# Attention over edges: sums in batches of six over two PSUM banks, and the softmax head turned on VectorE

## What is computed

```
h = (x @ W_i).reshape(n, 4, 32)                     # 4 heads
e = leaky(es[src] + ed[dst])                        # one score per edge and head
m = segment_max(e, dst); p = exp(e - m[dst])
out = segment_sum(p / segment_sum(p, dst)[dst] * h[src], dst) + b_i
```

## Time and profile before

| | us |
|---|---|
| median of the timed executions | 10107.16 |
| the profiled execution's own time | 10027.24 |
| its span, first to last instruction | 10025.4 |
| PE busy | 5468.7 (55%) |
| DVE busy | 5313.1 (53%) |
| ACT busy | 4632.0 (46%) |
| POOL busy | 4936.8 (49%) |
| POOL gathers (L706) | 4980 instructions, 4700.9 busy, 3010.1 idle before them |
| PE sums (L1275) | 9984 instructions, 2452.2 busy |
| DVE adds (L1993) | 4992 instructions, 1476.5 busy |

### The profile page before, as it was taken

The page is one execution under the profiler, slowest core; times in us unless marked ns, Lnnn a source line. Parts: engine busy times, 40 slices in busy tenths (PEclk is TensorE's granted clock), DMA queues, the critical chain, the costliest instruction groups (busy, mean ns, idle before and its releaser), DMA issues.

```text
span 10025.4 us, 128907 instructions
## 1 busy us (share of the span) xinstructions
PE 5468.7 (55%) x33764; PEld 4402.8 (44%) x33764; DVE 5313.1 (53%) x12476; ACT 4632.0 (46%) x8410; POOL 4936.8 (49%) x5153
## 2 busy tenths in 40 slices
PE   3999799635444444553544445444534444444446
PEld 2777566524444444442444444444423333333334
DVE  5888711335555555554555555555634444444445
ACT  2555300245555555553555555555434444444444
POOL 2000300156666666662666666666466666666660
PEclk9999899855555555555555555555555555555558
DMA  2333355134333333442333333433322222222221
GB/s 83 141 135 141 122 187 191 61 99 108 102 103 101 103 103 103 107 105 66 102 103 102 102 102 104 108 102 103 80 74 76 71 71 71 76 71 71 71 76 32
DMA packets 600500, 985.16 MB, mean 98 GB/s; under 512 B 330886, under 2 KB 454492, under 8 KB 560780
## 3 DMA queue, kind: packets, MB, share of 16 engines
q1 hardware_dynamic: 216924, 540.94, 16.0%
q0 software_dynamic: 163376, 356.21, 15.2%
q10 hardware_dynamic: 219648, 81.82, 3.1%
HBM read 755.78 MB, written 222.74 MB: 98 GB/s over the span
## 4 chain that ended last, share of the span: by engine, by line
PE 30%; DVE 22%; another core or an unknown queue 19%; DVEq 14%; issue 10%; ACT 3%; DMA 1%; ACTq 1%; POOL 0%; POOLq 0%; SPq 0%
PE bank L1040 12%; DVEq L1363 11%; DVE acc L1993 10%; PE bank L1275 8%; DVE arena L1980 3%; PE bank L1064 2%; PE bank L1215 2%; PE bank L1203 2%; DVE bank L1949 2%; DVEq L1993 2%; DVE arena L1951 1%; ACT pick_dist L863 1%; DVEq L1985 1%; PE bank L1346 1%
## 5 line engine op out<-in xcount | busy, mean ns | idle before, releaser
L706 POOL DMA_INDIRECT arena<-row_table,staged_idx x4980 | 4700.9, 944 | 3010.1 <-issue 1749.0
L1275 PE MATMUL bank<-arena 128*128 128x136 f32 x9984 | 2452.2, 424 | 1521.3 <-issue 729.0
L1275 PEld LDWEIGHTS bank<-arena 128*128 128x128 f32 x9984 | 2171.8, 312 | 1688.3 <-issue 1688.2
L1993 DVE TENSOR_TENSOR acc<-acc,bank 128x136 f32 x4992 | 1476.5, 296 | 2096.8 <-issue 822.5
L863 ACT ACTIVATE pick_dist<-col,dst_local 128x128 bf16<-128x128 f32 x4992 | 1521.8, 388 | 551.1 <-remote 419.6
L1040 PE MATMUL bank<-arena 128*128 128x385 bf16 (+1 forms) x7448 | 1325.5, 327 | 36.5 <-DVE arena L1733 20.0
L815 ACT COPY x_mem<-bank 128x384 f32<-128x384 f32 x416 | 198.9, 478 | 1619.1 <-remote 1001.5
L1040 PEld LDWEIGHTS bank<-arena 128*128 128x128 bf16 x7448 | 702.2, 98 | 458.1 <-issue 22.1
L1980 DVE TENSOR_TENSOR arena<-arena,bank 128x528 f32<-128x528 f32 x1248 | 831.9, 687 | 0.7
L648 POOL TENSOR_TENSOR arena<-acc,node_stat 128x896 f32 x14 | 23.9, 1708 | 1612.6 <-POOLq L660 987.5
L1215 PE MATMUL bank<-ident,x_mem 96*128 96x96 f32 x1664 | 365.7, 375 | 738.7 <-DVE x_mem L1641 494.0
(11 more groups left out here) (371 smaller groups left out, 5343.6 us busy)
## 6 DMA issues: line engine op xcount, KB each, us to landing
arena<-dst_rows SPq DMA_DIRECT2D x156, 1024.0 KB
cell_rows<-arena SPq DMA_DIRECT2D x75, 1568.0 KB, 5.1
arena<-cell_rows SPq DMA_DIRECT2D x75, 1568.0 KB, 6.5
edge_stats<-x_mem ACTq DMA_DIRECT2D x416, 192.0 KB
arena<-row_table,staged_idx POOLq DMA_INDIRECT x4980
x_mem<-in_edge_attr SPq DMA_DIRECT2D x208, 192.0 KB
x_mem<-segment_flags SPq DMA_DIRECT2D x416, 96.0 KB
arena<-change_rows SPq DMA_DIRECT2D x312, 64.0 KB
```

The costliest lines, as they stand in the source:

```text
L706: pool.indirect_dma_start(gathered[:, at, :], None, table, bass.IndirectOffsetOnAxis(staged_idx[:, at:at + 1], 0)).then_inc(att_gathered[n ...
L1275: mm = pe.matmul(region(k)[:, 0:ROW], pick[:, k, :], gathered[:, b * GROUP + k, :], start=True, stop=True)
L1993: done = dve.tensor_tensor(row, row, region(m * BATCH + k), ALU.add)
```

## The change

Batches have six slots (the last one of a group two), so a group has 6 batches. Three sums lie side by side in a PSUM bank, a batch takes two banks, and two batches (`HELD`) are in flight, 12 sums in place of 8. All turns of the softmax head leave PE: they become 32x32 block transposes on DVE, and with them go five semaphore pairs and PE's places for them. `score_rows` and `back` stay in bank 3. The orders of PE and DVE are written anew for six batches.

```diff
-BATCH = 4
+BATCH = 6
+HELD = 2
+BANK_SUMS = 3
-    STEPS = GROUP // BATCH + 1
+    NBATCH = -(-GROUP // BATCH)
+    STEPS = NBATCH + 1
+        score_rows = bank[0:GROUP, 3, :]
+        back = bank[:, 3, 0:P].rearrange("p (h s) -> p h s", h=HEADS)
+        row_ends = over(3840, GROUP, 2 * GROUP)
+        cross_rows = over(3840 + 2 * GROUP, GROUP, 2 * GROUP)
-        def region(k):
-            return bank[:, 4 + k % (2 * BATCH) // 2, k % 2 * ROW:(k % 2 + 1) * ROW]
+        def slots_of(m):
+            return range(m * BATCH, min((m + 1) * BATCH, GROUP))
+        def region(G, m, k):
+            at = k - m * BATCH
+            spot = BATCH // BANK_SUMS * ((G * NBATCH + m) % HELD) + at // BANK_SUMS
+            return bank[:, 4 + spot, at % BANK_SUMS * ROW:(at % BANK_SUMS + 1) * ROW]
...
-                            act.wait_ge(att.summed, (n * NG + g + 2) * NBATCH + (q + 1) * (ROUND // BATCH))
+                            act.wait_ge(att.summed, (n * NG + g + 2) * NBATCH - (-((q + 1) * ROUND) // BATCH))
...
                 def sum_batch(G, b, m):
...
-                    pe.wait_ge(att.added, G * STEPS + m + FREE + (1 if m >= 2 else 0))
+                    taken_group, taken_batch = divmod(G * NBATCH + m - HELD, NBATCH)
+                    if taken_group >= 0:
+                        pe.wait_ge(att.added, taken_group * STEPS + taken_batch + 2)
...
                     for m in range(NBATCH):
                         sum_batch(G, b, m)
-                        if head and m == 2 + late:
-                            turn_scores(G + 1)
...
-                        if n < STATS_LAYERS and m in (4, 5):
-                            scan_turn(n, g, 0, m - 4)
-                        if ahead and m == 5:
-                            score_some(0, 2, slot, (G + 2) * 2)
-                        if ahead and m == 6:
-                            score_some(2, 5, slot, (G + 2) * 2)
+                        if n < STATS_LAYERS and m in (3, 4):
+                            scan_turn(n, g, 0, m - 3)
+                        if ahead and m == 4:
+                            score_some(0, 3, slot, (G + 2) * 2)
...
+                def turn_scores():
+                    then()
+                    for q in range(P // GROUP):
+                        dve.transpose(score_rows_h[:, :, q * GROUP:(q + 1) * GROUP],
+                                      score[q * GROUP:(q + 1) * GROUP, :, :])
+                    then()
...
+                    dve.transpose(row_ends[:, 0:GROUP],
+                                  seg_f_h.rearrange("s h e -> s e h")[:, ::-1, :][:, 0:GROUP // HEADS, :])
+                    dve.transpose(row_ends[:, GROUP:2 * GROUP],
+                                  seg_m_h.rearrange("s h e -> s e h")[:, 0:GROUP // HEADS, :])
...
+                    dve.transpose(cross_rows, cross[:, :, :].rearrange("p m s -> p (m s)"))
...
+                def turn_maxima():
+                    then()
+                    for q in range(P // GROUP):
+                        dve.transpose(back[q * GROUP:(q + 1) * GROUP, :, :],
+                                      seg_m_h[:, :, q * GROUP:(q + 1) * GROUP])
+                    then()
...
-                    late = 0 if ahead else 3
+                    late = 0 if ahead else 2
                     for m in range(NBATCH):
-                        if m + 2 < NBATCH:
-                            weigh(G, b, m + 2)
+                        if m + HELD < NBATCH:
+                            weigh(G, b, m + HELD)
                         add_batch(G, slot, m)
                         if head and m == 0 + late:
                             score_edges(G + 1, 1 - b, use)
                         if head and m == 1 + late:
-                            first_scans(G + 1, 1 - b, use)
+                            turn_scores()
+                            first_scans(1 - b, use)
                         if head and m == 2 + late:
-                            carries(G + 1, 1 - b)
+                            carries(1 - b)
+                        if head and m == 2 + late:
+                            last_scans(1 - b)
                         if head and m == 3 + late:
-                            last_scans(G + 1, 1 - b)
-                        if head and m == min(5 + late, NBATCH - 1):
-                            shift_scores(G + 1, 1 - b, slot + GROUP)
-                        if n < STATS_LAYERS and m in (2, 6):
+                            turn_maxima()
+                            shift_scores(1 - b, slot + GROUP)
+                        if n < STATS_LAYERS and m in (1, 4):
                             scan_edges(n, g, m // 4)
```

More of the change, by code:

```diff
@@ L1219, in _ @@
                 if n == 0:
-                    pe.sem_inc(att.added, FREE_REGIONS)
                     pe.sem_inc(st.turned, 2 * FREE)
@@ L1263, in score_some @@
                 def score_some(first, last, slot, turned):
+                    if first == 0:
+                        pe.wait_ge(att.scored, turned // 2)
                     for j in range(first, last):
@@ L1950, in last_scans @@
                     then()
-                    dve.tensor_tensor_scan(seg_m[:, ::-1], end_flag[:, b, ::-1], grp[:, ::-1], FAR,
-                                           ALU.add, ALU.max).then_inc(att.maxima, 1)
-                def shift_scores(head, b, slot):
-                    dve.wait_ge(att.max_back, head + 1)
+                    dve.tensor_tensor_scan(seg_m[:, ::-1], end_flag[:, b, ::-1], score_rows[:, ::-1], FAR,
+                                           ALU.add, ALU.max)
+                def turn_maxima():
+                    then()
+                    for q in range(P // GROUP):
+                        dve.transpose(back[q * GROUP:(q + 1) * GROUP, :, :],
+                                      seg_m_h[:, :, q * GROUP:(q + 1) * GROUP])
+                    then()
@@ L1956, in shift_scores @@
+                def shift_scores(b, slot):
                     dve.tensor_tensor(score[:, :, :], score[:, :, :], back, ALU.subtract
@@ L1989, in add_batch @@
                     dve.sem_inc(dve_tick, 1)
-                    for k in range(BATCH):
-                        row = acc[:, bass.ds(at[k], ROW)]
+                    for k in slots:
+                        row = acc[:, bass.ds(at[k - m * BATCH], ROW)]
                         then()
-                        done = dve.tensor_tensor(row, row, region(m * BATCH + k), ALU.add)
+                        done = dve.tensor_tensor(row, row, region(G, m, k), ALU.add)
                     done.then_inc(att.added, 1)
@@ L2001, in dve_group @@
                     rescale(G, slot)
-                    weigh(G, b, 0)
-                    weigh(G, b, 1)
-                    late = 0 if ahead else 3
+                    for m in range(HELD):
+                        weigh(G, b, m)
+                    late = 0 if ahead else 2
                     for m in range(NBATCH):
-                        if m + 2 < NBATCH:
-                            weigh(G, b, m + 2)
+                        if m + HELD < NBATCH:
+                            weigh(G, b, m + HELD)
                         add_batch(G, slot, m)
@@ L2024, in _ @@
                 score_edges(n * NG, 0, 0)
-                first_scans(n * NG, 0, 0)
-                carries(n * NG, 0)
-                last_scans(n * NG, 0)
-                shift_scores(n * NG, 0, 0)
+                turn_scores()
+                first_scans(0, 0)
+                carries(0)
+                last_scans(0)
+                turn_maxima()
+                shift_scores(0, 0)
                 for it in range(PAIRS - 1):
```

110 lines of the change are left out of this document (34 added, 76 removed).

## The result

The changed kernel takes 10583.04 us (10560.48 to 10595.91, four runs) against 10105.10 us for the kernel before in the same job: 1.0471 times as long, interval 1.0452 to 1.049. The forecast was 9920. The execution profiled took 10577.04 us (span 10575.0), 550 us more than that of before.

A forecast was written before the change was run, and what follows sets the result against it. It took POOL's chain of gathers with its pauses, not DVE's or PE's work, as the bound. Terms -1.5 + 0.1 + 0.2 = -1.2 us a group over 156 groups gave -187 us: 10107 to 9920 us, range 9590 to 10230.

The forecast's parts named there:

- The gathers' chain with its pauses: POOL's 32 gathers a group: 39.8 us plus 8.7 us of pauses make the whole 48.5 us period.
- rival B: Gathers' pauses fall to two a group, runs of 18 and 14: -3.3 us a group, 9590 us; chance 0.13.
- The waits of DVE for turns: DVE's waits for PE's two middle turns, 7.6 us a group, go; counted as no gain.
- The turns' price: Block transposes on DVE: 0.3 us large, 0.2 small; +3.8 us of DVE work a group, costing 0.2 us.
- 2.8 x 2.58 = 7.2 us against 8.7: POOL's pauses: 2.8 a group at 2.58 us each with batches of six, a gain of 1.5 us a group.
- told-late result of PE: PE results late in a gather run are seen only after its last gather, then about 2.6 us of nothing.
- A longer run covers it: Moved scan and turns delay DVE's adds up to 4.5 us; a 15 us run of 12 gathers covers PE's queued batch.
- The weight of 0.06 for DVE's work: Each microsecond of DVE work a group, beside the gathers, adds about 0.06 us to the period.
- the second weighing: Weighing at a group's start, half as long again: DVE's first add about 1.1 us later, counted as 0.1 us.
- one for the head: Softmax head's turns moved from PE to DVE: +3.8 us of DVE work a group, counted as 0.2 us.
- Rival C: DVE sets the pace, with turns, scans and adds in one line: 50.0 us a group, 10340 us; chance 0.20.
- The prediction's last sentence: Signs of being wrong; the last is a pause over 2.6 us because DVE, not the hold, ends it.

The follow-up runs named there:

- e1_turns: Kernel before with only the softmax head's block transposes moved to VectorE, batches of four and before's places kept: 1.0014 of the kernel before.
- e2_quarters: Changed kernel with five quarters of scores behind batch 4 and three behind the second edge scan's turn, instead of three and five: 1.0318 of the kernel before.
- e3_scans: Changed kernel with the second edge scan behind batch 3 instead of 4, the first scan's turns behind batches 2 and 3: 1.0204 of the kernel before.
- e4_both: Changed kernel with the edits of e2_quarters and e3_scans together: 1.0098 of the kernel before.
- e13_fixed: Changed kernel with adds to 32 fixed rows, so no address loads or register steps ahead of them (output not the reference's): 1.0083 of the kernel before.
- e10_late: e1_turns with the second edge scan's turns behind the next group's batches 0 and 1, their ScalarE copies ahead of its first picks: 0.9917 of the kernel before.
- e9_cut: e4_both with a pause on GpSimd (three small memsets, each behind a drain) behind every eighth gather: 1.0840 of the kernel before.
- e7_half: Changed kernel with every second gather of a group left out (output not the reference's), a trace only: period 42.2 us a group in the first layer.

## Why the prediction was wrong

*The part that held.* The gathers' chain with its pauses sets the period: in each kernel with all its gathers the period is 39.8 us and the pauses. Pauses became fewer, 2.1 a group, nearly rival B's two, with the runs of 18 and 14 that B names. The waits of DVE for turns are gone. The turns' price was right: 0.316 to 0.322 us for the large ones (0.3 taken), 0.177 to 0.222 for the small (0.2), DVE's busy time up by 30.0 - 27.0 = 3.0 us a group. The Trainium skill (VectorE: DVE Perf Modes, The three transpose paths and The TRN2 errata) gave 0.29 by the prediction's estimate; the trace has a tenth more. In e1_turns that work cost +0.14%, as little as forecast.

*The step that failed* is the first of the change, "2.8 x 2.58 = 7.2 us against 8.7": a pause's length was taken from before as if it were a constant, and only their number was let vary. The measured product is 2.1 x 6.6 = 14 us in the first two layers and, over the third, some 2.2 x 3.9 = 8.6, where it was 8.5. The rows show that length varying. By the starts in the earlier trace rows the pauses at 3314.56 and 3326.80 stand behind runs of 8 gathers and are 2.2 and 2.3 us over the 0.30; the one at 3350.16 stands behind a run of 16 and is 3.4. The prediction took every run for one of 8 ("a run is 8 gathers") and the mean of 2.58 for each. In the changed kernel's third layer, with runs of up to 18 and 24, the mean was 3.9, and that alone ate up the gain. The loss comes on top, in the pause of 9.7 us at gather 0 of the first two layers. What the pauses hold is no longer a told-late result of PE but an operand that isn't made: the sums of batch 3 in the pause of 3.9 us wait for adds that came late, and the next group's first sums in the pause of 9.7 us for the adds, the scan and its turns.

*"A longer run covers it"* (behind the moved steps: PE's batch after next, "which the longer run (15 us for 12 gathers) covers") was wrong too. The run is not neutral cover. In the changed kernel the steps of the very work that it is to cover are slow towards its end.

*The weight of 0.06 for DVE's work* came from comparing layers of the kernel before, where VectorE has few long steps. In e1_turns it held, 4.4 us more issue time a group for 0.5 us; in the changed kernel 9.8 us more went with 5.1 us. Work is cheap where it lies under the gathers, and lateness at the group's end is not.

*A place not priced.* The prediction had a term for the second weighing and one for the head, none for the second edge scan's move from 28 slots to 30 and for the two more quarters between its turns. e2_quarters and e3_scans give the two 1.5 and 2.7 points, with the slow adds in place.

*Rival C* was on the right side with the wrong mechanism: DVE did not run out of time, it is idle for 23.6 of 53.6 us; it was slow to issue. The prediction's last sentence names the sign that appeared, a pause "longer than 2.6 us since DVE, not the hold, ends it", but no case was made of it and no chance given. Its sum is off as well: 40.3 + 5.1 + 2 x 2.6 is 50.6 us, not 50.0, so by its own terms C stood at some 10435 us, not 10340.

*Open.* Why a run of gathers slows other engines' steps isn't shown, nor why VectorE's are spared in the runs of 16 of the kernel before. Whether the held results of PE there are the same effect isn't shown either; the two end alike, though. The held results are told of 2.9 us behind the end of the run's last gather (3346.5 to 3349.4), and in the changed kernel the steps are fast again 2.7 us behind it (2467.4 to 2470.2). That the 1.0% left in e4_both is all slow adds wasn't tried apart: e13_fixed with e4_both's order would tell.

## What to carry to other kernels

A pause between runs of work is not overhead of fixed size: before counting fewer of them, sort the pauses you have by the run ahead of them, ask what each waits for, and what happens to that in a longer run. Where two engines' programs are written out by hand, count the slots between a late step and the next group's first; moving one step past that boundary (e10_late) brought 0.8%, and twelve sums in flight brought nothing. It is no rule either: in batches of six the same move did harm. When an engine's wait is taken away and its "issue" time grows in its place, the work did not get free.

## What the runs showed of the hardware

**Long runs of gathers slow the steps of other engines' instruction streams.** VectorE's register steps take 0.046 us in general, 0.70 in the median of the long ones and up to 1.4. In the changed kernel, with one indirect gather of GpSimd every 1.25 us, they are long in a quarter of the cases behind the seventh to eleventh gather in a row (200 of 790), and in 269 of 276 behind the fifteenth to eighteenth. A pause of 3.6 us after eight gathers prevents it (e9_cut, 19 long steps), and so does issuing half of them (e7_half, 21). Drains, waits for semaphores and loads of addresses get slow in the same stretches (0.70 to 0.73 us each between the adds at 2462.45 and 2470.21), and TensorE's register steps do too (147 of 4992 over 0.6 us in the kernel before, 349 in e13_fixed). A long run does not bring it every time: in the kernel before, with runs of 16, 3 of 109 of VectorE's steps behind the fifteenth gather are long. The adds themselves stay at 0.296 us and the gathers at 0.943 to 0.947, in all kernels.

The Trainium skill (SBUF — State Buffer, SBUF: two separate sides) has a rule for the two engines side by side: they contend for one pair of ports, as an exclusive lock that blocks the other's whole operation, and there VectorE holds up the making of GpSimd's transfers. Here it is VectorE that is held up, between its operations, and neither engine's data operations grew; no run here shows such a lock.

**A drain and a memset on GpSimd behind a gather begin 2 us late**: in e9_cut 2.0 us in the median (1.96 to 2.5 in nine of ten of 621) pass between the gather's end and the memset, so that a cheap break in a run isn't to be had that way. Which of the two costs it, no run parts.
